# A transformer block on one core: the score maxima taken on the whole TensorE array, head by head, in place of two 64-row tiles at once

## The chip, the cores and the metric

One NeuronCore of a Trainium2 chip runs the whole program in one launch. The metric is the device time in microseconds; the time before is the median of three runs.

## What is computed

The reference is a pre-norm block: attention with rotary embedding, then a mixture of experts that each take their best tokens. Only the attention is touched by the change.

```python
B, N, DIM, H = 8, 1024, 256, 16          # batch, tokens, width, heads
DH = DIM // H                            # 16
q, kv = split(x @ Wq), split(x @ Wkv)    # to (b*H, n, DH); keys and values are the same kv
q, kv = rotary(q) * DH ** -0.5, rotary(kv)
attn = softmax(einsum('bmd,bnd->bmn', q, kv), axis=-1)
out = einsum('bij,bjd->bid', attn, kv)
x = x + merge_heads(out) @ Wout + bout
# then LayerNorm, softmax gate, top-k tokens for each of 8 experts, gelu network, scatter-add
```

The softmax needs the largest score of each query before the exponentials can be taken: with 1024 keys for a query, in two chunks of 512.

## The kernel before, in words

The program has five stages, one after the other: `project` (queries, keys, values), `attend` (the attention), `finish`, `choose` and `experts`. The change is in `attend`, which takes two heads at a time, a "pair": 8 sequences x 8 pairs = 64 pairs.

A query or key vector of 16 numbers is held as three bf16 parts (0, 1, 2), whose sum is close to the f32 value. `SLOTS` lists six products of a query part with a key part, and so each head has six slots of 16 rows, 96 rows in all, in each of `qb` (tile `a_q`) and `kb` (tile `a_k`). One matmul over all of them sums the six products. Two further rows of `qb`, at `MAX_ROW`, hold the negated maxima of the queries in two bf16 parts, and the same rows of `kb` hold ones, so that the scores come out with their maximum taken off. The rest is zero.

TensorE has these kinds of work in a pair, which the texts below call by a letter:

- **S**, `scores` (L570): keys x queries with all 128 rows, 128x512 into tile `a_st`, three buffers. 32 in a pair, two for each of the 16 steps `g`; head `h = g % 2`.
- **M**, `maxima` (L597): queries x keys into tile `a_sm`, for a later pair. One M is two matmuls, one for each head, into two banks; 16 M in a pair, one for each step. Two M buffers, so that an M needs the reduce of the M two before it. Before the change head 0 uses rows 0 to 63 and head 1 rows 64 to 127, which hold the first four slots of each: two tiles of 64 rows of the array.
- **V**, `values` (L585): the probabilities x values, f32, on four tiles of 32 columns at once (two heads x two halves of the queries); the trace has 8 matmul records for one V. One V for every second step.
- **T**, `turn_maxima` (L603): one transpose in a pair, on a tile of 32 columns, of the split maxima; it uses a buffer of `a_sm`. ScalarE copies its result (L741), and the next M (of step 12) must not start before the copy is done.

The order on TensorE is written out by hand in `body`:

```python
for g in range(NG):                       # 16 steps
    scores(q, g, 0)
    if g == TURN_AT + 1: unit(TURN_AT)    # TURN_AT = 12
    if g % 2 == 1 and g >= 3: values(q, (g - 3) // 2)
    ...
    if g == TURN_AT: turn_maxima(q.plus(1))
    scores(q, g, 1)
    if g != TURN_AT: unit(g)              # the maxima M of a later pair
```

Two steps make a cycle, S M S S M S V, which stands seven times in a pair; the steps 12 and 13 differ: S M S T S S M V. VectorE reduces each M to its maxima (L660), and once in a pair joins two halves (L668). ScalarE takes the exponential of each S (L727), copies V's sum out once in a pair (L734), and copies T's result. GpSimd splits the maxima and places the values. SyncE issues the loads of a pair (L520, L526), its store and the two rows of maxima (L538).

Before the first pair a prologue takes the first pair's 16 M and 8 M of the second, with no S or V between them. The last pair has no M to take ahead, and the last but one has half of them: so 64 x 16 - 24 = 1000 M stand between S and V in the bodies of the pairs, and 62 T.

Of the kernel before, what the change touches and what calls it, by code (L numbers as in the profile page):

```python
# [25 lines left out]
P = 128  # L26
# [380 lines left out]
SLOTS = ((0, 0), (1, 1), (0, 1), (1, 0), (2, 0), (0, 2))  # L407


SLOT_ROW = ([0, 16, 32, 48, 64, 80], [64, 80, 96, 112, 0, 16])  # L410
MAX_ROW = (96, 32)
MAX_PARTS = 2


def slot_runs(h, kind):

    runs = []
    for row, of in zip(SLOT_ROW[h], SLOTS):
        part = of[kind]
        if runs and runs[-1][0] + runs[-1][2] * DH == row and runs[-1][1] + runs[-1][2] == part:  # L420
            runs[-1][2] += 1
        else:
            runs.append([row, part, 1])
    return runs
# [6 lines left out]
def attend(nc, parts_dram, v_dram, o_dram, ident_d):  # L431
# [7 lines left out]
    with ExitStack() as ctx:  # L439
# [3 lines left out]
        qb = a.sb("a_q", [P, 3, 2, N], BF16)  # L443
# [31 lines left out]
        pv_done = a.sem("a_pv_done")  # L475
        evac_done = a.sem("a_evac_done")
        block = ctx.enter_context(nc.Block())
        QK_LOADS = sum(len(slot_runs(h, kind)) for h in range(2) for kind in range(2))
        UNITS = 2 * NG
        AHEAD = NG + NG // 2  # L480

# [29 lines left out]
        @block.sync  # L511
        def _(sp):
            def load(q):
                if not (q.p is not None and q.p < 3):

                    sp.wait_ge(st_done, (q.n - 2) * UNITS)
                for h in range(2):
                    for kind, buf in ((0, qb), (1, kb)):
                        for row, part, parts in slot_runs(h, kind):
                            sp.dma_start(buf[row:row + parts * DH, q.buf, h, :],  # L520
                                         parts_dram[bass.ds(q.n * 2 + h, 1), kind, part:part + parts]
                                         .rearrange("o s d n -> (o s d) n")).then_inc(qk_in[q.buf], 16)
                if not (q.p is not None and q.p < 3):

                    sp.wait_ge(v_placed, q.n - 2)
                sp.dma_start(v_raw[:, q.buf].rearrange("p i h e -> p (i h e)"),  # L526
                             v_dram[bass.ds(q.n, 1)].rearrange("o p n -> (o p) n")).then_inc(v_in[q.buf], 16)

            def store(q):
                sp.wait_ge(evac_done, q.n + 1)  # L530
                sp.dma_start(o_dram[bass.ds(q.n, 1)].rearrange("o h c r n -> (o h c r) n"), oraw[:]).then_inc(o_out, 16)

            def max_rows(q):

                sp.wait_ge(mrow_done, q.n + 1)
                rows = MAX_PARTS * TILES
                for h in range(2):
                    sp.dma_start(qb[MAX_ROW[h]:MAX_ROW[h] + MAX_PARTS, q.buf, h, :].rearrange("r (t c) -> r t c", c=P),  # L538
                                 mrow[h * rows:(h + 1) * rows, :]).then_inc(m_in, 16)

            def body(q):
                if not q.first() and q.plus(2).exists():
                    load(q.plus(2))
                if not q.first():
                    store(q.plus(-1))
                if q.plus(1).exists():
                    max_rows(q.plus(1))

            sp.dma_start(identf[:], ident_d).then_inc(ident_in, 16)
            for p in range(3):  # L550
                load(Pair(0, p, p))
            sp.wait_ge(set_up, 8)
            max_rows(Pair(0, 0, 0))
            pairs(sp, body)
            store(Pair(0, NP - 1, NP - 1))
            sp.wait_ge(o_out, 16 * NP)

        @block.tensor
        def _(pe):
            def scores(q, g, ic):  # L560

                jt, h = g // 2, g % 2
                u = g * 2 + ic
                slot = (q.c * UNITS + u) % 3
                if g == 0 and ic == 0:
                    pe.wait_ge(m_in, (q.n + 1) * 32)
                if not (q.first() and u < 3):

                    pe.wait_ge(exp_done, q.n * UNITS + (u - 2))
                nc.tensor.matmul(st[:, slot], kb[:, q.buf, h, jt * P:(jt + 1) * P],  # L570
                                 qb[:, q.buf, h, ic * CHUNK:(ic + 1) * CHUNK],
                                 start=True, stop=True).then_inc(st_done, 1)

            def values(q, jt):

                if jt == 0:
                    pe.wait_ge(v_placed, q.n + 1)
                    if not q.first():

                        pe.wait_ge(evac_done, q.n)  # L580
                pe.wait_ge(exp_done, q.n * UNITS + 4 * jt + 4)
                for h in range(2):
                    for ic in range(HALVES):
                        row = 2 * DH * (h * HALVES + ic)
                        mm = nc.tensor.matmul(pv[row:row + 2 * DH, :], vb[:, q.buf, jt, h, :],  # L585
                                              prob[:, (2 * jt + h) % 4, ic * CHUNK:(ic + 1) * CHUNK],
                                              start=(jt == 0), stop=(jt == TILES - 1))
                mm.then_inc(pv_done, 1)

            def maxima(q, v, slot):  # L590

                qt, kc = v // 2, v % 2
                if v == 0:
                    pe.wait_ge(qk_in[q.buf], (q.turn + 1) * 16 * QK_LOADS)
                for h in range(2):
                    rows = slice(64 * h, 64 * h + 64)
                    mm = nc.tensor.matmul(sm[:, slot, h], qb[rows, q.buf, h, qt * P:(qt + 1) * P],  # L597
                                          kb[rows, q.buf, h, kc * CHUNK:(kc + 1) * CHUNK], start=True, stop=True)
                mm.then_inc(sm_done, 1)

            def turn_maxima(q):
                pe.wait_ge(n2_done, q.n + 1)
                nc.tensor.transpose(turned, nsplit[:].rearrange("p h s t -> p (h s t)"), identb[:]).then_inc(mT_done, 1)  # L603

            def body(q):
                seen = q.n * NG + AHEAD

                def unit(g):
                    ahead = q.plus(1) if g < NG // 2 else q.plus(2)
                    if ahead.exists():  # L610

                        pe.wait_ge(max_done, seen + g - 1)
                        if g == TURN_AT:

                            pe.wait_ge(mrow_done, q.n + 2)
                        maxima(ahead, (g + NG // 2) % NG, g % 2)

                for g in range(NG):
                    scores(q, g, 0)
                    if g == TURN_AT + 1:  # L620
                        unit(TURN_AT)
                    if g % 2 == 1 and g >= 3:
                        values(q, (g - 3) // 2)
                    elif g == 1 and not q.first():
                        values(q.plus(-1), TILES - 1)
                    if g == TURN_AT and q.plus(1).exists():
                        if q.plus(2).exists():
                            pe.wait_ge(max_done, seen + g - 1)
                        turn_maxima(q.plus(1))
                    scores(q, g, 1)  # L630
                    if g != TURN_AT:
                        unit(g)

            q0, q1 = Pair(0, 0, 0), Pair(0, 1, 1)
            for v in range(NG):
                if v >= 2:
                    pe.wait_ge(max_done, v - 1)
                maxima(q0, v, v % 2)
            pe.wait_ge(identb_set, 1)
            turn_maxima(q0)  # L640
            for v in range(NG // 2):
                pe.wait_ge(max_done, NG + v - 1)
                if v == 0:

                    pe.wait_ge(mrow_done, 1)
                maxima(q1, v, v % 2)
            pe.wait_ge(set_up, 8)
            pairs(pe, body)
            values(Pair(0, NP - 1, NP - 1), TILES - 1)
# [70 lines left out]
        def _(act):  # L720
# [32 lines left out]

            for buf in (kb, qb):
                for h in range(2):
                    rows = slice(MAX_ROW[h], MAX_ROW[h] + 32)
                    nc.scalar.copy(buf[rows, :, h], zero[rows, 0:1, 0:1].to_broadcast([32, 3, N])).then_inc(set_up, 1)
            act.wait_ge(set_up, 6)

            for h in range(2):  # L760
                rows = slice(MAX_ROW[h], MAX_ROW[h] + MAX_PARTS)
                nc.scalar.copy(kb[rows, :, h], vb[rows, 0, 0, 0:1, DH:DH + 1].to_broadcast([MAX_PARTS, 3, N])
                               ).then_inc(set_up, 1)
            copy_max_rows(Pair(0, 0, 0))
# [1135 lines left out]
```

## Time and profile before

| What | Value |
|---|---|
| Time of the three runs | 2557.94 us median, 2556.48 to 2560.4 |
| Span of the profiled execution, which its own time is here taken to be | 2556.1 us |
| PE busy over the span | 2193.1 us, 86% |
| DVE busy | 2025.9 us, 79% |
| ACT busy | 1539.9 us, 60% |
| POOL busy | 700.3 us, 27% |
| Reduces of M on DVE (L660) | 1024, mean 1220 ns |
| Exponentials on ACT (L727) | 2048, mean 600 ns |
| Granted clock, mean | 0.940 |

PE is TensorE, PEld its weight loads, DVE VectorE, ACT ScalarE, POOL GpSimd, SP SyncE. A matmul's record shows its own duration, and matmuls that follow one another overlap: what one costs in a stream is the distance from its start to the next one's start, not its duration. The execution's own time is not given apart from its span, which lies 1.8 us under the median of the three runs. The attention is the stretch from some 282 to 1776 us. The clock is 0.50 where TensorE runs at 1.2 GHz and 1.00 where it runs at 2.4 GHz.

### The profile page before, as it was taken

How to read it: one execution, taken by the hardware profiler on the slowest of the kernel's cores; microseconds unless marked ns; L12 is line 12 of the kernel's file. 1: busy time of each engine (PE TensorE's matmuls, PEld its weight loads, DVE VectorE, ACT ScalarE, POOL GpSimd, SP SyncE). 2: the span in 40 equal slices, each digit the busy share in tenths (PEclk: the TensorE clock that was granted, in tenths of full speed). 3: DMA queues.
4: the chain of work that ended last, by engine and by line, in shares of the span. 5: the costliest groups of instructions: out<-in, count | busy, mean ns of one | idle time of the engine just before them, and what ended most of it. 6: DMA issues, size and time to landing. Idle time of an engine off the chain costs nothing. (4 is left out here: it accounts for less than half of the span.)

```text
span 2556.1 us, 46500 instructions
## 1 busy us (share of the span) xinstructions
PE 2193.1 (86%) x12567; PEld 911.7 (36%) x12716; DVE 2025.9 (79%) x3221; ACT 1539.9 (60%) x2920; POOL 700.3 (27%) x846
## 2 busy tenths in 40 slices
PE   6766299999999999999999999997589317999898
PEld 3333022222222222222222222221355216888888
DVE  8999488888888888888888888882467677888774
ACT  4556277777777777777777777776133103344333
POOL 7899000000000000000000000000377214666664
PEclk9999599999999999999999999999699658999999
DMA  2554412111121111111111111111675213334332
GB/s 83 172 175 153 132 38 56 49 49 51 56 56 49 50 50 56 56 50 50 50 56 56 50 50 49 56 56 37 160 237 189 78 53 81 74 75 94 78 73 31
DMA packets 154359, 198.91 MB, mean 78 GB/s; under 512 B 28451, under 2 KB 98598, under 8 KB 154278
## 3 DMA queue, kind: packets, MB, share of 16 engines
q1 hardware_dynamic: 141990, 180.92, 23.2%
q0 software_dynamic: 12288, 17.05, 4.1%
q8 instruction: 35, 0.57, 0.1%
q14 instruction: 46, 0.38, 0.0%
HBM read 121.06 MB, written 76.28 MB: 77 GB/s over the span
## 5 line engine op out<-in xcount | busy, mean ns | idle before, releaser
L660 DVE TENSOR_REDUCE a_mx<-a_sm 128x2 f32<-128x1024 f32 x1024 | 1216.8, 1220 | 232.3 <-PE a_sm L597 222.1
L727 ACT ACTIVATE a_prob<-a_st 128x512 f32<-128x512 f32 x2048 | 1112.5, 600 | 299.2 <-PE a_st L570 244.1
L570 PE MATMUL a_st<-a_q,a_k 128*128 128x512 bf16 x1899 | 660.6, 387 | 13.1 <-issue 10.2
L585 PE MATMUL a_pv<-a_prob,a_v 128*32 128x512 f32 x4096 | 545.6, 605 | 11.4 <-ACT a_prob L727 11.0
L597 PE MATMUL a_sm<-a_k,a_q 64*128 64x512 bf16 x2048 | 404.9, 392 | 57.1 <-DMA a_k<-qkv_parts 34.8
L570 PEld LDWEIGHTS a_st<-a_q,a_k 128*128 128x128 bf16 x2048 | 156.0, 96 | 655.5 <-ACT a_prob L727 437.9
L703 POOL TENSOR_TENSOR a_v<-a_v_raw,a_zero 128x256 f32<-128x256 f32 x64 | 39.6, 619 | 1226.5 <-DMA a_v_raw<-values 1226.5
L1736 ACT ACTIVATE e_hT<-e_ps_h,e_b1b 128x512 f32<-128x512 f32 x128 | 88.1, 689 | 276.3 <-PE e_ps_h L1770 265.8
L597 PEld LDWEIGHTS a_sm<-a_k,a_q 64*128 64x128 bf16 x2048 | 99.9, 93 | 385.7 <-issue 215.7
L1770 PE MATMUL e_ps_o<-e_w_high,e_hT_high 128*128 128x256 f32 x512 | 151.6, 296 | 29.9 <-DVE e_biased L1641 29.9
L1629 DVE TENSOR_TENSOR e_hT_low<-e_hT,e_hT_high 128x512 fp32r<-128x512 f32 x128 | 120.7, 965 | 52.8 <-ACT e_hT_high L1742 37.3
L1770 PE MATMUL e_ps_o<-e_w_high,e_hT_low 128*128 128x256 f32 x512 | 149.3, 292 | 0.5 <-issue 0.5
L1770 PE MATMUL e_ps_o<-e_w_low,e_hT_high 128*128 128x256 f32 x512 | 149.3, 292 | 0.0
L383 PE MATMUL p_ps_q<-p_w,p_xnT 128*128 128x512 f32 x256 | 126.6, 619 | 0.0
L585 PEld LDWEIGHTS a_pv<-a_prob,a_v 128*32 128x32 f32 x4096 | 80.6, 108 | 117.1 <-ACT a_prob L727 86.2
L302 POOL TENSOR_TENSOR p_tsin<-p_qkv,p_sin 128x256 f32<-128x256 f32 x128 | 114.0, 910 | 3.2 <-ACT p_qkv L341 3.2
L1206 PE MATMUL f_ps_y<-f_w,f_o 128*128 128x256 f32 x256 | 80.7, 442 | 39.6 <-POOL f_o L981 39.2
L1770 PEld LDWEIGHTS e_ps_o<-e_w_high,e_hT_high 128*128 128x128 f32 x512 | 103.1, 201 | 32.0 <-DVE e_biased L1641 31.2
L1718 POOL DMA_INDIRECT out_dram<-e_ob,e_idx x64 | 107.6, 1681 | 17.4 <-issue 11.7
L1770 PEld LDWEIGHTS e_ps_o<-e_w_low,e_hT_high 128*128 128x128 f32 x512 | 103.1, 201 | 0.3
L1770 PEld LDWEIGHTS e_ps_o<-e_w_high,e_hT_low 128*128 128x128 f32 x512 | 102.8, 201 | 0.0
L1770 PE MATMUL e_ps_h<-e_yT_high,e_w_high 128*128 128x512 f32 x256 | 101.3, 396 | 0.8 <-DVE e_yT_low L1605 0.7
(153 smaller groups left out, 2436.0 us busy)
## 6 DMA issues: line engine op xcount, KB each, us to landing
qkv_parts<-p_parts SPq DMA_DIRECT2D x96, 256.0 KB
a_k<-qkv_parts SPq DMA_DIRECT2D x512, 32.0 KB, 1.7
attended<-a_oraw SPq DMA_DIRECT2D x64, 256.0 KB, 2.2
e_w<-in_fc_dram SPq DMA_DIRECT2D x16, 1024.0 KB
a_q<-qkv_parts SPq DMA_DIRECT2D x192, 64.0 KB, 1.8
token_table<-f_tab SPq DMA_DIRECT2D x8, 1056.0 KB, 8.0
p_x<-in_x_dram SPq DMA_DIRECT2D x16, 512.0 KB, 5.4
values<-p_values SPq DMA_DIRECT2D x8, 1024.0 KB, 8.3
```

The costliest lines, as they stand in the source:

```text
L302: nc.gpsimd.tensor_tensor(ts[:, :, h * HALF:(h + 1) * HALF], src[:, :, (1 - h) * HALF:(2 - h) * HALF], sinb[:, i:i + 1, h * HALF:(h + 1) * ...
L383: mm = nc.tensor.matmul(ps_q[:, k % 2], xnT[:, k % 2, c], w[:, c], start=(c == 0), stop=(c == DC - 1))
L570: nc.tensor.matmul(st[:, slot], kb[:, q.buf, h, jt * P:(jt + 1) * P], qb[:, q.buf, h, ic * CHUNK:(ic + 1) * CHUNK], start=True, stop=True) ...
L585: mm = nc.tensor.matmul(pv[row:row + 2 * DH, :], vb[:, q.buf, jt, h, :], prob[:, (2 * jt + h) % 4, ic * CHUNK:(ic + 1) * CHUNK], start=(jt ...
L597: mm = nc.tensor.matmul(sm[:, slot, h], qb[rows, q.buf, h, qt * P:(qt + 1) * P], kb[rows, q.buf, h, kc * CHUNK:(kc + 1) * CHUNK], start=Tr ...
L660: nc.vector.tensor_reduce(mx[:, qt, kc, :], sm[:, slot], AX.X, ALU.max, negate=True).then_inc(max_done, 1)
L727: nc.scalar.activation(prob[:, g % 4, ic * CHUNK:(ic + 1) * CHUNK], st[:, (q.c * UNITS + u) % 3], ACT.Exp, scale=DH ** -0.5).then_inc(exp_ ...
L1206: nc.tensor.matmul(ps_y[:, k % 2, 0:D], o[:, s, ch, i * P:(i + 1) * P], w[:, ch], start=(ch == 0), stop=False)
L1629: nc.vector.tensor_tensor(group_of(hT_low, g), hT[:, g % 4], group_of(hT_high, g), ALU.subtract).then_inc(hT_low_done, 1)
L1718: nc.gpsimd.indirect_dma_start(out=out_rows, out_offset=bass.IndirectOffsetOnAxis(ap=idx[:, k, i:i + 1], axis=0), in_=ob[:, i], in_offset= ...
L1736: nc.scalar.activation(hT[:, g % 4], ps_h[:, g % 3], ACT.Gelu_apprx_tanh, bias=b1b[:, k, g % FC:g % FC + 1]).then_inc(gelu_done, 1)
L1770: return nc.tensor.matmul(to, weights, moving, start=first, stop=last)
```

## The change

Both heads now use the same layout, six slots in rows 0 to 95 and the maxima at row 96. An M is still two matmuls, but each reads the 96 rows of its head from row 0 and takes the whole array. So an M sums six products where it summed four. Nothing else on TensorE, VectorE, ScalarE or GpSimd stands in another place; head 1's zeros and ones are written to rows 96 to 127 and 96 to 97.

```diff
-SLOT_ROW = ([0, 16, 32, 48, 64, 80], [64, 80, 96, 112, 0, 16])
-MAX_ROW = (96, 32)
+SLOT_ROW = [0, 16, 32, 48, 64, 80]
+DATA_ROWS = 96
+MAX_ROW = 96
 MAX_PARTS = 2
 
-def slot_runs(h, kind):
+def slot_runs(kind):
 
     runs = []
-    for row, of in zip(SLOT_ROW[h], SLOTS):
+    for row, of in zip(SLOT_ROW, SLOTS):
...
-        QK_LOADS = sum(len(slot_runs(h, kind)) for h in range(2) for kind in range(2))
+        QK_LOADS = 2 * sum(len(slot_runs(kind)) for kind in range(2))
...
-                        for row, part, parts in slot_runs(h, kind):
+                        for row, part, parts in slot_runs(kind):
...
-                    sp.dma_start(qb[MAX_ROW[h]:MAX_ROW[h] + MAX_PARTS, q.buf, h, :].rearrange("r (t c) -> r t c", c=P),
+                    sp.dma_start(qb[MAX_ROW:MAX_ROW + MAX_PARTS, q.buf, h, :].rearrange("r (t c) -> r t c", c=P),
                                  mrow[h * rows:(h + 1) * rows, :]).then_inc(m_in, 16)
...
                 for h in range(2):
-                    rows = slice(64 * h, 64 * h + 64)
+                    rows = slice(0, DATA_ROWS)
                     mm = nc.tensor.matmul(sm[:, slot, h], qb[rows, q.buf, h, qt * P:(qt + 1) * P],
                                           kb[rows, q.buf, h, kc * CHUNK:(kc + 1) * CHUNK], start=True, stop=True)
                 mm.then_inc(sm_done, 1)
```

On SyncE's queue the loads of a pair change, because a run of slots that are neighbours in rows and in parts is one DMA. Before, at the first pair of the prologue (`a_q` are the queries, `a_k` the keys, head 0 and then head 1):

```order
87 L520 DMA a_q<-qkv_parts 32x1024
88 L520 DMA a_q<-qkv_parts 48x1024
89 L520 DMA a_q<-qkv_parts 16x1024
90 L520 DMA a_k<-qkv_parts 32x1024
91 L520 DMA a_k<-qkv_parts 16x1024 x4
92 L520 DMA a_q<-qkv_parts 32x1024 x2
93 L520 DMA a_q<-qkv_parts 16x1024 x2
94 L520 DMA a_k<-qkv_parts 32x1024
95 L520 DMA a_k<-qkv_parts 16x1024 x4
```

And in the changed program, at the same place:

```order
87 L521 DMA a_q<-qkv_parts 32x1024
88 L521 DMA a_q<-qkv_parts 48x1024
89 L521 DMA a_q<-qkv_parts 16x1024
90 L521 DMA a_k<-qkv_parts 32x1024
91 L521 DMA a_k<-qkv_parts 16x1024 x4
92 L521 DMA a_q<-qkv_parts 32x1024
93 L521 DMA a_q<-qkv_parts 48x1024
94 L521 DMA a_q<-qkv_parts 16x1024
95 L521 DMA a_k<-qkv_parts 32x1024
96 L521 DMA a_k<-qkv_parts 16x1024 x4
```

Head 1's four loads of queries became three, so a pair has 16 loads of queries and keys in place of 17. On TensorE nothing moves. Its order in the first pair, at steps 9 to 13, is this in the changed program (where line numbers are higher by one), and the same in the one before:

```order
198 L571 MATMUL a_st<-a_q,a_k 128x512
199 L598 MATMUL a_sm<-a_k,a_q 128x512 x2
```

```order
204 L571 MATMUL a_st<-a_q,a_k 128x512
205 L598 MATMUL a_sm<-a_k,a_q 128x512 x2
206 L571 MATMUL a_st<-a_q,a_k 128x512
207 L604 MATMUL a_sm<-a_identb,a_nsplit 32x128
208 L571 MATMUL a_st<-a_q,a_k 128x512 x2
209 L598 MATMUL a_sm<-a_k,a_q 128x512 x2
210 L586 MATMUL a_pv<-a_prob,a_v 32x512 x4
211 L571 MATMUL a_st<-a_q,a_k 128x512
212 L598 MATMUL a_sm<-a_k,a_q 128x512 x2
```

The first piece is the S and M of step 9; the second begins with the S and M after step 11's V and shows the T, the two S, and the M of step 12 right ahead of step 13's V. What the order can't show is that the two matmuls of an M stood on tiles of 64 rows before and stand on the whole array now, as S does.

## Rows read from the trace of the kernel before

**Rows 1.** Windows: stretch, PE, PEld, DVE, ACT, POOL busy, clock, DMA share, GB/s.
```profile
306.00:320.00 14.00, 6.34 (x23) 1.16 (x23) 11.76 (x12) 0.25 (x1) 1.15 (x3) 0.50 0.08 20
...
338.00:1728.00 1390.00, 1359.54 (x7729) 326.41 (x7870) 1171.72 (x1038) 1094.04 (x2075) 70.52 (x183) 1.00 0.18 52
```

**Rows 2.** Timeline of one cycle: start, length, what, count, idle before it.
```profile
1001.12 0.39 PE L570 MATMUL a_st<-a_q,a_k 128*128 128x512 bf16 x1
...
1001.45 0.39 PE L597 MATMUL a_sm<-a_k,a_q 64*128 64x512 bf16 x2
1001.55 2.30 ACT L727 ACTIVATE a_prob<-a_st 128x512 f32<-128x512 f32 x4 [0.40 <-PE a_st L570]
...
1001.77 0.60 PE L570 MATMUL a_st<-a_q,a_k 128*128 128x512 bf16 x2
1001.88 2.36 DVE L660 TENSOR_REDUCE a_mx<-a_sm 128x2 f32<-128x1024 f32 x2 [0.42 <-PE a_sm L597]
...
1002.31 0.39 PE L597 MATMUL a_sm<-a_k,a_q 64*128 64x512 bf16 x2
...
1002.63 0.39 PE L570 MATMUL a_st<-a_q,a_k 128*128 128x512 bf16 x1
...
1002.95 1.06 PE L585 MATMUL a_pv<-a_prob,a_v 128*32 128x512 f32 x8
1003.94 0.10 PEld L570 LDWEIGHTS a_st<-a_q,a_k 128*128 128x128 bf16 x1 [0.84 <-ACT a_prob L727]
```

**Rows 3.** Timeline of PE at the first and the last T of 62.
```profile
338.42 0.23 PE L603 MATMUL a_sm<-a_identb,a_nsplit 128*32 128x128 bf16 x1
...
1728.09 0.23 PE L603 MATMUL a_sm<-a_identb,a_nsplit 128*32 128x128 bf16 x1
```

**Rows 4.** Timeline around one T, steps 11 to 13.
```profile
1020.88 0.39 PE L570 MATMUL a_st<-a_q,a_k 128*128 128x512 bf16 x1
...
1021.84 0.23 PE L603 MATMUL a_sm<-a_identb,a_nsplit 128*32 128x128 bf16 x1
...
1022.19 0.25 ACT L741 COPY a_mrow<-a_sm 32x128 bf16<-32x128 bf16 x1 [0.28 <-PE a_sm L603]
1022.23 0.38 PE L570 MATMUL a_st<-a_q,a_k 128*128 128x512 bf16 x1 [0.16 <-issue]
...
1022.59 0.39 PE L597 MATMUL a_sm<-a_k,a_q 64*128 64x512 bf16 x2
...
1023.91 0.39 PE L570 MATMUL a_st<-a_q,a_k 128*128 128x512 bf16 x1
```

**Rows 5.** Timeline of PE in the last pair, where no M stands.
```profile
1744.86 0.82 PE L570 MATMUL a_st<-a_q,a_k 128*128 128x512 bf16 x3
1745.62 1.07 PE L585 MATMUL a_pv<-a_prob,a_v 128*32 128x512 f32 x8
```

**Rows 6.** Timeline: M of step 7, and the reduces of steps 8 and 9.
```profile
1038.34 0.39 PE L597 MATMUL a_sm<-a_k,a_q 64*128 64x512 bf16 x2
...
1040.33 2.49 DVE L660 TENSOR_REDUCE a_mx<-a_sm 128x2 f32<-128x1024 f32 x2
```

**Rows 7.** Timeline of PE in the prologue, two M.
```profile
306.71 0.61 PE L597 MATMUL a_sm<-a_k,a_q 64*128 64x512 bf16 x2 [0.53 <-DVE a_mx L660]
...
307.85 0.61 PE L597 MATMUL a_sm<-a_k,a_q 64*128 64x512 bf16 x2 [0.52 <-DVE a_mx L660]
```

**Rows 8.** Timeline of SP: the loads of queries, head 0 and head 1.
```profile
281.99 1.35 SPq L520 DMA_DIRECT2D a_q<-qkv_parts  x3
...
285.69 1.81 SPq L520 DMA_DIRECT2D a_q<-qkv_parts  x4
```

**Rows 9.** The page's first line.
```profile
span 2556.1 us, 46500 instructions
```

**Rows 10.** Timeline of PE in the experts' stage: two matmuls, fourteen starts apart.
```profile
2299.72 0.39 PE L1770 MATMUL e_ps_h<-e_yT_high,e_w_high 128*128 128x512 f32 x1
...
2302.90 0.39 PE L1770 MATMUL e_ps_h<-e_yT_high,e_w_low 128*128 128x512 f32 x1
```

More of the change, by code:

```diff
@@ L755, in _ @@
                 for h in range(2):
-                    rows = slice(MAX_ROW[h], MAX_ROW[h] + 32)
+                    rows = slice(MAX_ROW, MAX_ROW + 32)
                     nc.scalar.copy(buf[rows, :, h], zero[rows, 0:1, 0:1].to_broadcast([32, 3, N])).then_inc(set_up, 1)
@@ L760, in _ @@
             for h in range(2):
-                rows = slice(MAX_ROW[h], MAX_ROW[h] + MAX_PARTS)
+                rows = slice(MAX_ROW, MAX_ROW + MAX_PARTS)
                 nc.scalar.copy(kb[rows, :, h], vb[rows, 0, 0, 0:1, DH:DH + 1].to_broadcast([MAX_PARTS, 3, N])
```

## The prediction

> **What bounds the kernel now.** I read the windows first. Between 338 and 1728 us TensorE shows work in 1359.5 of 1390 us at a granted clock of 1.00, VectorE in 1171.7 and ScalarE in 1094.0 [rows 1]. The reader should see that TensorE has no idle time left there, while the other two have a sixth or more.
>
> Then the timeline of one cycle, S M S S M S V [rows 2]. From start to start it goes 0.33 (S to M), 0.32 (M to S), 0.54 (both S, to M), 0.32 (M to S), 0.32 (S to V) and 0.99 (V to the weight load of the next S): 2.82 us. In it VectorE's two reduces take 2.36 and ScalarE's four exponentials 2.30. No wait of TensorE stands in these rows. The whole is very regular: from the first T at 338.42 to the last at 1728.09 there are 61 distances, 22.78 us each [rows 3]; the section with T, from the S at 1020.88 to the one at 1023.91, is 3.03 [rows 4], and 7 x 2.82 + 3.03 = 22.77. So a change of TensorE's time per cycle comes out of the total as it is, up to the point where VectorE or ScalarE takes over.
>
> **The price of changing tiles.** A lone S costs 0.32 to the next kind, two S 0.54 [rows 2], and three S, in the last pair where no M stands, 1745.62 - 1744.86 = 0.76 [rows 5]. The slope is (0.76 - 0.32) / 2 = 0.22; 512 columns at 2.4 GHz would be 0.213, and the three S as one row of 0.82 against the lone 0.39 give (0.82 - 0.39) / 2 = 0.215. I take 0.216 for each further matmul. The rest of the 0.32, 0.105, is paid at each change from one kind of tile to another. An M before the change costs 0.32 for both its matmuls, so these run side by side and a change of tile follows.
>
> The Trainium skill ("TensorEngine Tiling (Array Packing)", Key Properties) says that a change of tiling mode, and not of the tile alone, drains TensorE; the 0.105 us in the trace agree.
>
> **The change, part by part.** *Ordinary M.* Of the 1000 M in the bodies, 938 stand between two S. The change removes two changes of tile at each, 2 x 0.105 = 0.21, and adds one matmul that no longer runs beside the other, 0.216. A cycle has eight matmuls in one run, 0.32 + 7 x 0.216 = 1.83, then V with 0.99 to 1.00: 2.83 against 2.82. By the thousandth the balance is below what the rows resolve; I take +4 to +5 ns for each M (+9 ns a cycle): 938 x 0.0045 = +4.2 us. So nearly all the array time that is added comes back as changes of tile not made.
>
> *The M of step 12.* It stands between S and V, so the change of tile behind it stays. The one ahead of it is no gain either: this M waits for ScalarE's copy of T's result. The copy ends at 1022.19 + 0.25 = 1022.44, and M starts at 1022.59, 0.15 later and 0.75 after T; the S ahead of it starts at 1022.23, and M comes 0.36 behind it instead of the 0.31 to 0.32 of other places [rows 4]. On one tile it could start at 0.216 behind that S, but the copy is no earlier, so it stays at 0.75 after T. What is queued behind it is V and all that follows. It then has its second matmul: +0.216. 62 x 0.216 = +13.4 us. Its neighbour M of step 11 is an ordinary one.
>
> *The waits that this could wake.* VectorE's result of an M comes 0.22 later, since its second matmul ends later. The tightest place is step 10, as VectorE joins the halves after step 7's reduce: step 8's reduce starts 1040.33 - 1038.34 = 1.99 after step 7's M [rows 6]. After the change it is 2.21, its end at 1.22 more 3.43, and M of step 10 could follow at some 3.58 (the 0.15 of above). In the new order V starts 1.62 after step 7's M, the next S 1.00 later, and step 10's M 5 x 0.216 after that, 3.70. So 0.12 us of slack; hidden, and if the cover were missing by 0.1 it would cost 62 x 0.1 = 6 us. ScalarE: an exponential starts 0.43 after its S (1001.55 - 1001.12); its four take 2.30 of 2.83, and in the new order the S come at 0, 0.65, 0.86 and 1.51, so it is never more than one behind. Three buffers of `a_st` cover that. I cost both at nothing.
>
> *Prologue.* The clock is 0.50 there [rows 1], M follow each other at 1.14 us [rows 7], the pace of VectorE. At 1.2 GHz 512 columns take 0.43, so the second matmul ends 0.43 later: 0.15 + 0.61 + 0.43 + some 0.1 to the reduce is 1.29 after a buffer comes free, where 1.14 is allowed. That can cost up to 24 x 0.15 / 2 = 2 us, as each wait delays two buffers. Against it, TensorE works nearly twice as long there and its clock may rise sooner, which would take the second off and some 2 us from the first steps of the first pair. I take 0, with 2 us either way.
>
> *Loads.* Head 1's queries come in 3 DMAs instead of 4: 1.81 against 1.35 on SP's queue [rows 8]. Ahead of the first M this is on the path: -0.45 us. In the loop SP's loads lie two pairs ahead and give nothing. The first setting of zeros and ones has the same sizes: nothing.
>
> Sum: 4.2 + 13.4 - 0.45 = +17.2 us on the span of 2556.1 [rows 9]: 2573.3. The median lies 1.8 above that span, so I forecast 2575 us. A difference of 0.2% (5 us) is about what a measurement of this kernel tells from none.
>
> **The rivals.**
>
> *A longer pitch in long runs (a).* The rows show S runs of three at most in bf16. In the experts' stage, where runs are long, matmuls of 512 columns follow at (2302.90 - 2299.72) / 14 = 0.227 [rows 10]. Those are f32 in name and their weights may load more slowly, so S is nearer kin. At 0.227 a cycle has 7 x 0.011 = 0.08 more, a pair 0.6: 62.5 x 0.6 = 37, in all some 2612 us.
>
> *96 rows are not taken as the whole array (b).* Then all changes of tile stay and each M is 0.216 longer: 1000 x 0.216 = +216, 2774 us. No matmul of 96 rows stands in the trace. The Trainium skill ("TensorEngine Tiling (Array Packing)", Available Configurations) lists rows in 128, 64 or 32, which speaks against a kind of its own for 96.
>
> *The weight loads come into the open (c).* Two M matmuls use other weights on the same rows. Loads take 0.10 [rows 2]; six of a cycle's seven gaps change weights: 0.6 a cycle, some 4.6 a pair, +290: some 2865 us. Against it: in the run of three S the third has other weights than the second and still comes at 0.216 [rows 5].
>
> The Trainium skill ("TensorE: Matmul & The Clock Gate", What overlaps and what doesn't) has this rule, that a weight load overlaps a running matmul only on other rows. By it the sum would be (c)'s; the run of three speaks against it.
>
> *The copy does not hold step 12's M (d).* Should the release be quicker on the same tile, 0.15 a pair is won back: -9 us, 2566 us.
>
> *Faster (e).* One mechanism could do it: a pitch below 0.216 in one run on one tile. The loss of 0.28 a pair is spread over some 53 gaps in runs, so from 0.211 down the kernel is faster than before. Were it far below, VectorE would bound at 8 x 2.36 + 0.3 = 19.2 a pair, and the time would be 62.5 x 3.6 = 225 less, 2333. Against it: the gaps of 0.215 to 0.22, and 0.213 for 512 columns at 2.4 GHz.
>
> The Trainium skill ("TensorE: Matmul & The Clock Gate", Back-to-back issue gap) gives some 131 ns as the spacing sustained in streams of 512 columns, which would be this case; no row here shows it.
>
> *No change (f).* The prologue gains its 2 us, step 12 its 9, and the ordinary M come out at nothing instead of +4: within 0.2%.
>
> **How the numbers follow.** The forecast 0.66 (its own range 2567 to 2584: the step-10 slack, the prologue, and 4 ns for each M), (a) 0.10, (b) 0.05, (c) 0.03, (d) 0.07, (e) 0.04, (f) 0.05. The range of 2564 to 2613 takes in the forecast, (a) and (d), and leaves out (b), (c), (e) and most of (f). Slower by over 0.2%: 0.66 + 0.10 + 0.05 + 0.03 + 0.07 = 0.91; within: 0.05; faster: 0.04.
>
> **What would show it.** In the profile after: S and M as one run of eight at 0.22 from start to start, then V; a cycle of 2.83; from T to T 23.06 instead of 22.78; step 12's M still 0.75 after T, with ScalarE's copy as its releaser, and V 0.54 behind it. PE busy over 338 to 1728 stays near 98%. A wait for VectorE at step 10's M would show the slack to be gone. A gap of 0.23 or more inside a run is (a), of 0.32 ahead of M (b), of 0.31 where weights change (c). A clock over 0.50 between 306 and 320 shows the early rise. The prediction is wrong if a cycle is not within 0.02 of 2.83.

## The result and the profile after

The changed kernel takes 2577.55 us (median of five runs, 2573.96 to 2580.74) against 2560.4 for the kernel before, now that it has five runs too. The ratio is 1.0069, with a 95% interval of 1.005 to 1.0087: slower by 0.7%, 13 to 22 us. The forecast was 2575.

The page's first line, its line on TensorE and those of the three kinds of TensorE's work and of VectorE's reduces (line, operation, tiles, count, busy us and mean ns, idle before):

```profile
span 2576.1 us, 46465 instructions
...
PE 2249.4 (87%) x12716; PEld 1001.3 (39%) x12716; DVE 2025.8 (79%) x3221; ACT 1539.4 (60%) x2920; POOL 700.4 (27%) x846
...
L661 DVE TENSOR_REDUCE a_mx<-a_sm 128x2 f32<-128x1024 f32 x1024 | 1217.8, 1221 | 250.8 <-PE a_sm L598 239.9
...
L571 PE MATMUL a_st<-a_q,a_k 128*128 128x512 bf16 x2048 | 698.1, 382 | 2.6 <-ACT a_prob L728 2.6
L598 PE MATMUL a_sm<-a_k,a_q 96*128 96x512 bf16 x2048 | 620.9, 384 | 38.1 <-DMA a_k<-qkv_parts 34.2
L586 PE MATMUL a_pv<-a_prob,a_v 128*32 128x512 f32 x4096 | 545.5, 605 | 0.8 <-ACT a_prob L728 0.7
```

M's records cover 620.9 us where they covered 404.9: its two matmuls no longer lie on one another. VectorE waits 18 us longer for M in all (239.9 against 222.1), which is the kernel's loss seen from an engine that does the same work as before.

The windows, with the columns of [rows 1]:

```profile
306.00:320.00 14.00, 10.10 (x22) 1.93 (x21) 11.36 (x11) 0.71 (x2) 0.53 (x2) 0.50 0.01 2
320.00:326.00 6.00, 6.00 (x31) 2.01 (x33) 5.01 (x5) 4.71 (x10) 0.00 (x0) 0.88 0.00 0
...
338.00:1728.00 1390.00, 1390.00 (x7772) 407.67 (x7764) 1156.52 (x1024) 1079.54 (x2048) 69.41 (x180) 1.00 0.18 51
```

TensorE is busy for the whole of the long stretch. The 1359.54 of [rows 1] can't be set against this: the trace before has records for only 1899 of its 2048 S, the trace after for all of them. VectorE and ScalarE have less to do in the stretch than in [rows 1], because fewer steps fit in.

One cycle on TensorE, which answers to [rows 2]:

```profile
1501.16 0.39 PE L571 MATMUL a_st<-a_q,a_k 128*128 128x512 bf16 x1
1501.39 0.60 PE L598 MATMUL a_sm<-a_k,a_q 96*128 96x512 bf16 x2
1501.82 0.60 PE L571 MATMUL a_st<-a_q,a_k 128*128 128x512 bf16 x2
1502.26 0.59 PE L598 MATMUL a_sm<-a_k,a_q 96*128 96x512 bf16 x2
1502.69 0.38 PE L571 MATMUL a_st<-a_q,a_k 128*128 128x512 bf16 x1
1503.00 1.07 PE L586 MATMUL a_pv<-a_prob,a_v 128*32 128x512 f32 x8
1504.00 0.39 PE L571 MATMUL a_st<-a_q,a_k 128*128 128x512 bf16 x1
```

From S to M there is now 0.23 where there was 0.33, and from M to S 0.43 where there was 0.32. The steps are 0.23, 0.43, 0.44, 0.43, 0.31, 1.00: 2.84 us, against 2.82. The first four are the seven distances inside the run of eight matmuls, 1.53 / 7 = 0.219 each.

The section with T, which answers to [rows 4]:

```profile
1027.78 0.39 PE L571 MATMUL a_st<-a_q,a_k 128*128 128x512 bf16 x1
...
1028.44 0.38 PE L571 MATMUL a_st<-a_q,a_k 128*128 128x512 bf16 x1
...
1028.75 0.23 PE L604 MATMUL a_sm<-a_identb,a_nsplit 128*32 128x128 bf16 x1
...
1028.91 0.60 PE L571 MATMUL a_st<-a_q,a_k 128*128 128x512 bf16 x2
1029.09 0.25 ACT L742 COPY a_mrow<-a_sm 32x128 bf16<-32x128 bf16 x1 [0.29 <-PE a_sm L604]
...
1029.49 0.59 PE L598 MATMUL a_sm<-a_k,a_q 96*128 96x512 bf16 x2
...
1030.01 1.07 PE L586 MATMUL a_pv<-a_prob,a_v 128*32 128x512 f32 x8
...
1031.01 0.39 PE L571 MATMUL a_st<-a_q,a_k 128*128 128x512 bf16 x1
```

T to M is 0.74 (0.75 before), M to V 0.52 (0.32 before), and the section is 3.23 against 3.03. The first and the last T, as in [rows 3]:

```profile
L604 PE MATMUL a_sm<-a_identb,a_nsplit x62: 229/229/230, 336.4 to 1744.3; 128*32 128x128 bf16 x62
```

(1744.3 - 336.4) / 61 = 23.08 from T to T, 0.30 more than 22.78. Over 62 pairs that is 18.6 us.

### The profile page after: what moved, and what is told of

It reads as the page before. It is cut to its first block and busy times, and to the rows that moved or that the text cites. A ratio compares the mean times of both kernels' runs of the same rounds, so it can differ in the third digit from the quotient of the medians.

```text
span 2576.1 us, 46465 instructions
## 1 busy us (share of the span) xinstructions
PE 2249.4 (87%) x12716; PEld 1001.3 (39%) x12716; DVE 2025.8 (79%) x3221; ACT 1539.4 (60%) x2920; POOL 700.4 (27%) x846
## 5 line engine op out<-in xcount | busy, mean ns | idle before, releaser
L661 DVE TENSOR_REDUCE a_mx<-a_sm 128x2 f32<-128x1024 f32 x1024 | 1217.8, 1221 | 250.8 <-PE a_sm L598 239.9
L571 PE MATMUL a_st<-a_q,a_k 128*128 128x512 bf16 x2048 | 698.1, 382 | 2.6 <-ACT a_prob L728 2.6
L598 PE MATMUL a_sm<-a_k,a_q 96*128 96x512 bf16 x2048 | 620.9, 384 | 38.1 <-DMA a_k<-qkv_parts 34.2
L571 PEld LDWEIGHTS a_st<-a_q,a_k 128*128 128x128 bf16 x2048 | 191.5, 96 | 608.6 <-ACT a_prob L728 436.9
L598 PEld LDWEIGHTS a_sm<-a_k,a_q 96*128 96x128 bf16 x2048 | 195.2, 98 | 250.0 <-DMA a_k<-qkv_parts 34.6
```

Source lines behind the costliest of these rows:

```text
L661: nc.vector.tensor_reduce(mx[:, qt, kc, :], sm[:, slot], AX.X, ALU.max, negate=True).then_inc(max_done, 1)
```

## The experiments

The comparisons below are with runs of the kernel before on the same chip, 2557.42 us for the first four and 2559.07 for the last two. For each kernel the last line of its section gives the first and the last of 62 T, and so the time of a pair, which is finer than the total.

### M on 64 rows, one head after the other

```diff
                 for h in range(2):
-                    rows = slice(0, DATA_ROWS)
+                    rows = slice(0, 64)
```

> The changed kernel, with each matmul of an M reading rows 0 to 63 of its head instead of 0 to 95 (four products are summed, as before the change; both heads on the same 64-row tile, one after the other). My theory (what counts is the tile, 0.105 us at each change, and 0.216 for each matmul that no longer runs beside another): the changes of tile come back at 938 ordinary M, 2 x 0.105 each, +197 us on the changed kernel, some 2774 us, a cycle of 3.26. Rival (the change costs because 96 rows are streamed instead of 64): faster than the changed kernel, near the time before, 2558.

Measured: 2772.87 us, ratio 1.0845 (1.0824 to 1.0867). Its timeline of TensorE:

```profile
1501.38 0.39 PE L571 MATMUL a_st<-a_q,a_k 128*128 128x512 bf16 x1
1501.70 0.60 PE L598 MATMUL a_sm<-a_k,a_q 64*128 64x512 bf16 x2
1502.23 0.60 PE L571 MATMUL a_st<-a_q,a_k 128*128 128x512 bf16 x2
1502.77 0.60 PE L598 MATMUL a_sm<-a_k,a_q 64*128 64x512 bf16 x2
1503.31 0.39 PE L571 MATMUL a_st<-a_q,a_k 128*128 128x512 bf16 x1
1503.63 0.64 PE L586 MATMUL a_pv<-a_prob,a_v 128*32 128x512 f32 x4
```

```profile
L604 PE MATMUL a_sm<-a_identb,a_nsplit x62: 230/230/230, 341.5 to 1937.4; 128*32 128x128 bf16 x62
```

The matmuls sit 0.22 apart as in the changed kernel, but S to M takes 0.32 again instead of 0.23, and M to S 0.53 instead of 0.43. A pair is 26.16. This kernel stands between the two and splits the change: to run M's matmuls one after the other costs 26.16 - 22.78 = 3.38 a pair; to have them on S's tile gives back 26.16 - 23.08 = 3.08, at 15 M with two changes each 0.205, or 0.103 a change. Fewer rows streamed gave nothing: the rival's 2558 is out.

### M on 80 rows

```diff
-                    rows = slice(0, DATA_ROWS)
+                    rows = slice(0, 80)
```

> The changed kernel, with each matmul of an M reading rows 0 to 79 instead of 0 to 95 (five products are summed instead of six). My theory (more than 64 rows is the whole array, and the number of rows costs nothing): the same time as the changed kernel, 2577 within 5 us, 23.08 from T to T. Rival (each row of operands costs): a third to a half of the way back to the time before, 2568 to 2570.

Measured: 2577.04 us, ratio 1.0073 (1.0052 to 1.0094). T:

```profile
L604 PE MATMUL a_sm<-a_identb,a_nsplit x62: 229/229/230, 339.1 to 1747.0; 128*32 128x128 bf16 x62
```

A pair is 23.08, as with 96 rows. With the run on 64 rows this says that between 64 and 80 rows the tile changes and the price with it, and that between 80 and 96 nothing does.

### A third matmul in M

```diff
-                for h in range(2):
+                for h in (0, 1, 1):
                     rows = slice(0, DATA_ROWS)
```

> The changed kernel, with head 1's matmul of each M issued twice into the same place, so that an M is three matmuls (the result is the same). My theory (a further matmul of 512 columns in a run costs 0.216 to 0.218 at full clock): 1000 x 0.217 = +217, and up to 6 more in the prologue, some 2794 to 2800 us. Rival (matmuls of one run overlap further than the distance of 0.216 tells, at some 0.13 each): +131, 2708.

Measured: 2800.05 us, ratio 1.0943 (1.092 to 1.0966). T:

```profile
L604 PE MATMUL a_sm<-a_identb,a_nsplit x62: 229/229/229, 345.1 to 1963.5; 128*32 128x128 bf16 x62
```

A pair is 26.53, 3.45 more than the changed kernel's, and 3.45 / 16 = 0.216 for each matmul. Repeated matmuls of one run do not overlap beyond that, and the runs of ten have the same distance as those of eight. That ends the rival of 0.13 each.

### T's result copied twice

```diff
+        mrow_idle = a.sb("a_mrow_idle", [2 * MAX_PARTS * TILES, P], BF16)
...
+                nc.scalar.copy(mrow_idle[:], turned)
                 nc.scalar.copy(mrow[:], turned).then_inc(mrow_done, 1)
```

> The changed kernel, with ScalarE copying T's result twice, first into a tile that nobody reads, and releasing only after the second. My theory (step 12's M is held by this copy at 0.75 after T, and V and all behind it wait with it): the second copy starts 0.17 to 0.25 later, and the whole of that comes into each of 62 pairs, 23.26 to 23.33 from T to T, +11 to +16 us, 2588 to 2593. Rival (the copy is not what ends last there, but TensorE's own order, with 0.1 us or more to spare): +0 to +8 us.

Measured: 2583.44 us, ratio 1.0106 (1.0088 to 1.0123). Its timeline behind T:

```profile
1032.81 0.23 PE L605 MATMUL a_sm<-a_identb,a_nsplit 128*32 128x128 bf16 x1
...
1033.15 0.26 ACT L743 COPY a_mrow_idle<-a_sm 32x128 bf16<-32x128 bf16 x1 [0.29 <-PE a_sm L605]
1033.32 0.25 ACT L744 COPY a_mrow<-a_sm 32x128 bf16<-32x128 bf16 x1
...
1033.71 0.59 PE L599 MATMUL a_sm<-a_k,a_q 96*128 96x512 bf16 x2
```

```profile
L605 PE MATMUL a_sm<-a_identb,a_nsplit x62: 229/229/229, 335.7 to 1753.2; 128*32 128x128 bf16 x62
```

The second copy starts 0.17 behind the first, M is 0.90 after T instead of 0.74, and a pair is 23.24, 0.16 longer: the delay goes through whole, which it could not with 0.1 us to spare. So the copy does hold step 12's M. In size I was above it: 62 x 0.16 = 10 us, not 11 to 16. The medians alone (+6 us, or +9 when each is set against its own runs of the kernel before) would not have told the theories apart, since the rival's range reached to 8 and mine began at 11; the distance of the T does.

### The new order S S V S S M M, on 64-row tiles

If a change of tile costs 0.10 and two M in a row run at hardly more than their own 0.22 each, then the kernel before should gain by an order with fewer changes. The first two pieces are TensorE's, the last one ScalarE's.

```diff
-    TURN_AT = 12
+    TURN_AT = 10
...
-                for g in range(NG):
-                    scores(q, g, 0)
-                    if g == TURN_AT + 1:
-                        unit(TURN_AT)
-                    if g % 2 == 1 and g >= 3:
-                        values(q, (g - 3) // 2)
-                    elif g == 1 and not q.first():
-                        values(q.plus(-1), TILES - 1)
-                    if g == TURN_AT and q.plus(1).exists():
-                        if q.plus(2).exists():
-                            pe.wait_ge(max_done, seen + g - 1)
-                        turn_maxima(q.plus(1))
-                    scores(q, g, 1)
-                    if g != TURN_AT:
-                        unit(g)
+                for g in range(0, NG, 2):
+                    scores(q, g, 0)
+                    scores(q, g, 1)
+                    if g >= 2:
+                        values(q, (g - 2) // 2)
+                    elif not q.first():
+                        values(q.plus(-1), TILES - 1)
+                    if g == TURN_AT and q.plus(1).exists():
+                        if q.plus(2).exists():
+                            pe.wait_ge(max_done, seen + g - 1)
+                        turn_maxima(q.plus(1))
+                    scores(q, g + 1, 0)
+                    scores(q, g + 1, 1)
+                    unit(g)
+                    unit(g + 1)
...
-                    if g == 2 and not q.first():
+                    if g == 1 and not q.first():
                         evacuate(q.plus(-1))
-                    if g == TURN_AT and q.plus(1).exists():
+                    if g == TURN_AT + 1 and q.plus(1).exists():
                         copy_max_rows(q.plus(1))
```

> The kernel before, with its 64-row tiles, and the order of two steps changed from S S M S V S M to S S V S S M M, T behind the V of steps 10 and 11, ScalarE's copies of V's sum and of T's result moved accordingly. My theory (each change of tile costs 0.105): four changes in a cycle instead of six, 2.82 - 0.21 = 2.61, of which VectorE takes some back, since the second M of a cycle has to wait for a reduce that starts 1.14 after the first one's: a cycle of 2.65 to 2.70; T on V's tile costs 0.06 instead of 0.25. A pair 21.4 to 21.9, 2475 to 2505 us. Rival (two M in a row find both buffers held by VectorE, so that the wait eats what the tiles give): a cycle of 2.82 or more, 2555 us or over.

Measured: 2473.34 us, ratio 0.9645 (0.9617 to 0.9674): 3.5% faster than the kernel before, and faster than both kernels of this case. Like the kernel before, it sums four products in an M. One of its cycles:

```profile
1010.30 0.61 PE L570 MATMUL a_st<-a_q,a_k 128*128 128x512 bf16 x2
...
1010.84 0.60 PE L597 MATMUL a_sm<-a_k,a_q 64*128 64x512 bf16 x4
...
1011.27 2.36 DVE L660 TENSOR_REDUCE a_mx<-a_sm 128x2 f32<-128x1024 f32 x2 [0.27 <-PE a_sm L597]
...
1011.38 0.61 PE L570 MATMUL a_st<-a_q,a_k 128*128 128x512 bf16 x2
...
1011.91 1.06 PE L585 MATMUL a_pv<-a_prob,a_v 128*32 128x512 f32 x8
...
1012.91 0.11 PEld L570 LDWEIGHTS a_st<-a_q,a_k 128*128 128x128 bf16 x2 [0.84 <-ACT a_prob L727]
```

```profile
L603 PE MATMUL a_sm<-a_identb,a_nsplit x62: 219/219/219, 331.9 to 1634.7; 128*32 128x128 bf16 x62
```

Two M, four matmuls, take 1011.38 - 1010.84 = 0.54 to the next S, as long as two S; a cycle is 2.61 to 2.63 where I had 2.65 to 2.70, so VectorE takes back less than I gave it. VectorE still has 0.27 idle between its pairs of reduces. A pair is 21.36, 1.42 less than before, and 62 x 1.42 = 88 us, where the medians differ by 86. The pair and the time lie just below my ranges. The rival, that both buffers would be held, is out.

Once in a pair the first V of a new pair comes late:

```profile
1023.71 0.58 ACT L734 COPY a_oraw<-a_pv 128x512 f32<-128x512 f32 x1 [0.15 <-PE a_pv L585]
1024.19 2.07 ACT L727 ACTIVATE a_prob<-a_st 128x512 f32<-128x512 f32 x4
```

```profile
1024.59 0.65 PE L570 MATMUL a_st<-a_q,a_k 128*128 128x512 bf16 x2
1025.34 1.06 PE L585 MATMUL a_pv<-a_prob,a_v 128*32 128x512 f32 x8
```

It starts 0.75 behind the first of the two S ahead of it, and not 0.53 as elsewhere. It needs exponentials that ScalarE took only behind its copy of the last pair's sum. So this order still gives away some 0.22 a pair, by estimate 62 x 0.22 = 14 us, which the expectation did not have. No run here took that wait away.

### The same order on the whole array

The same edits, on the changed kernel.

> The changed kernel, whole array for M, with the same new order S S V S S M M and T behind V. My theory (M and S share a tile, so that two M in a row save no change; what is saved is T's own two changes, 0.2, and the hold of 0.14 on one M): a cycle still of 2.83 to 2.84, a pair 22.7 to 22.8, 2553 to 2560 us. Rival (the new order gains for another reason than tiles, such as where the exponentials fall): as much gained as on the kernel before in the same order, 70 us or so.

Measured: 2571.43 us, ratio 1.0032 (1.0014 to 1.0049). T, the V ahead of it and what follows:

```profile
1020.84 1.06 PE L586 MATMUL a_pv<-a_prob,a_v 128*32 128x512 f32 x8
...
1021.72 0.22 PE L604 MATMUL a_sm<-a_identb,a_nsplit 128*32 128x128 bf16 x1
...
1021.88 0.60 PE L571 MATMUL a_st<-a_q,a_k 128*128 128x512 bf16 x2
1022.09 0.25 ACT L742 COPY a_mrow<-a_sm 32x128 bf16<-32x128 bf16 x1 [0.19 <-PE a_sm L604]
...
1022.48 0.81 PE L598 MATMUL a_sm<-a_k,a_q 96*128 96x512 bf16 x3
```

```profile
L604 PE MATMUL a_sm<-a_identb,a_nsplit x62: 219/219/219, 335.8 to 1730.6; 128*32 128x128 bf16 x62
```

A pair is 22.87: 0.21 less than the changed kernel's. That the order gains 0.21 a pair where M and S share a tile, and 1.42 where they don't, is the contrast that I wanted. The 0.21 can be read at T: from V to the next S it takes 1021.88 - 1020.84 = 1.04, where it takes 1.00 with no T between. So T costs 0.04 here and 0.25 between two S in the changed kernel. But pair and time were missed: I had 22.7 to 22.8 and 2553 to 2560. What T saves came as forecast (0.2), but the hold of 0.14 on one M stayed: there are two S between T and M in this order too, and M again comes 0.76 after T, 0.14 behind the copy's end. The spans show less than 62 x 0.21 = 13 us: 2570.3 is 5.8 under the changed kernel's. From the first M to the last V it is 11.1 shorter (1491.95 against 1503.01), and in the stages before and behind, whose code is the same, 5.3 longer.

## Why the prediction was right

**The balance of an ordinary M**: right in kind and nearly in size. I had 0.216 for a matmul more, and the third matmul measured 0.216. I had 0.105 for each change of tile, and the run on 64 rows measured 0.103. What I sized a little low is the run of eight: its starts lie 0.219 apart on average, not 0.216. The mean cycle is (23.08 - 3.23) / 7 = 2.836, and before it was (22.78 - 3.03) / 7 = 2.821, so ordinary M cost 0.30 - 0.20 = 0.10 a pair where I had 0.06, and 6 us in all, not 4.

**Step 12's M**: right, and the largest term. Its section went from 3.03 to 3.23, and the way from this M to V alone from 0.32 to 0.52: 0.20 a pair, 12 to 13 us, for the 13.4 forecast. M stays 0.74 after T as forecast (0.75), and the doubled copy shows that the copy holds it. This one M in sixteen carries two thirds of the loss.

**Waits**: none woke, as forecast. In the stretch from 338 to 1728 no idle time of TensorE is left. I had its busy share near 98%; the idle 2% of [rows 1] were the S without a record.

**Prologue**: the step is right, the net a little off. The first M and the first S on TensorE's timeline of the changed kernel:

```profile
288.19 1.89 PE L598 MATMUL a_sm<-a_k,a_q 96*128 96x512 bf16 x4 [34.18 <-DMA a_k<-qkv_parts]
...
318.87 1.06 PE L571 MATMUL a_st<-a_q,a_k 128*128 128x512 bf16 x2
```

From the one to the other it takes 30.68 us, where the kernel before took 320.35 - 291.21 = 29.14, so 1.5 more: at a clock of 0.50 the second matmul ends 0.43 later, and VectorE came to wait for every second M. Its reduces start 1.18 apart on average, where they started 1.13 to 1.14 apart before. The early rise of the clock did not show where I had looked for it, between 306 and 320 us (0.50, as before). It came in the first pair: 0.88 between 320 and 326 us against 0.55, and from the first S to the first of the 62 T 17.49 instead of 18.07. I had the two cancel, within 2 us; together they are +1.0.

**Loads**: the first M came 3.0 us earlier in the profiled execution, but all but some 0.3 of it lay before the attention, in code that is the same. So -0.45 was about -0.3.

**The sum**: 18.6 + 1.0 - 0.3 = 19.3 for 17.2 forecast. The two traces bear this out: from the first M to the last V (1791.2 against 1774.7) the changed kernel takes 19.5 longer, the 18.6 and 1.0. The spans differ by 20.0, because the first M came 3.0 earlier and the stages behind the attention took 3.5 longer. The medians differ by 17.15. That this is the 17.2 of the forecast nearly to the digit is luck: the parts add up to 2 us more, and the measured difference itself is known only to between 13 and 22 us.

**The rivals**: a pitch of 0.227 (a) is not there, 0.216 to 0.22 stands; (b) and (c) are out by the cycle itself; (d) by the 0.74 and the doubled copy; (e) by the third matmul; (f) by the interval, which begins at 1.005. The Trainium skill's rule on weight loads ("TensorE: Matmul & The Clock Gate", What overlaps and what doesn't), by which (c) would hold, does not fit this trace: M's two matmuls have other weights on the same rows and come 0.22 apart. Nor does the spacing of some 131 ns that the Trainium skill gives for streams of 512 columns (the same page, Back-to-back issue gap): here they stand at 0.216.

Two slips in the description change no number: the last but one pair has a T too, so the bodies have 63 T, while step 12's M are 62; and the three S of [rows 5] stand in the second half of that pair, not in the last one.

## What to carry to other kernels

Count changes of tile on TensorE as work: each costs about half of a 512-column bf16 matmul at full clock. To put small matmuls on the big tile only trades these changes against the side-by-side running that it gives up; to group the small ones behind one another keeps both, and here it brought 3.5% where the trade lost 0.7%. The trade did buy something: six products in an M instead of four. Look for the one place in the loop where a wait sets the time: there a saved change gives nothing, while a matmul more counts in full.

## What I had not expected of the hardware

That two pairs of 64-row matmuls in a row take 0.54 to the next kind of work, exactly what two full ones do, with four weight loads that never show in the distances. And that T directly behind V, on a tile of the same 32 columns, costs so little: between two S, in the changed kernel, it takes 0.31 + 0.16 where 0.22 would stand without it, 0.25 in all. In the new order it adds 0.04 to the way from V to S, and the pair became 0.21 shorter. That it is the shared tile, and not another thing about this place, was not tried by itself.
